# Two-layer transformer kernel: the projection stage taken apart and issued inside the attention program

## What is computed

```python
def _L0_attn_ref(x, w_qkv, w_out, b_out):        # causal attention, 16 heads
    q, k, v = jnp.split(x @ w_qkv, 3, axis=-1)
    ...
    attn = jax.nn.softmax(dots, axis=-1)
def _L0_ffn_ref(x, W_up, W_gate, W_down):
    def ternary_quant(w):
        scale = jnp.mean(jnp.abs(w)) + EPS
        q = jnp.clip(jnp.round(w / scale), -1.0, 1.0) * scale
    ...
def _L1_attn_ref(x, Wq, Wkv, Wo, bo):            # 16 query heads, 4 key heads, linear bias, window mask
    cw = jax.nn.sigmoid(jnp.sum(jnp.abs(x), axis=-1, keepdims=True))
    q = jnp.dot(x * cw, Wq)
    kv = jnp.dot(x, Wkv)
    ...
x = _layernorm(x + _L0_attn_ref(...)); x = _layernorm(x + _L0_ffn_ref(...))
x = _layernorm(x + _L1_attn_ref(...)); x = _layernorm(x + _L1_ffn_ref(...))
```

## Time and profile before

| | before |
|---|---|
| median of three runs | 1176.63 us |
| the profiled execution, its own time | 1173.83 us |
| its span, first to last instruction | 1172.1 us |
| mean granted TensorE clock | 0.942 |
| busy: TensorE, VectorE, ScalarE, GpSimd | 88%, 62%, 51%, 28% |

### The profile page before, as it was taken

The page is one execution under the profiler, slowest core; times in us unless marked ns, Lnnn a source line. Parts: engine busy times, 40 slices in busy tenths (PEclk is TensorE's granted clock), DMA queues, the critical chain, the costliest instruction groups (busy, mean ns, idle before and its releaser), DMA issues. The chain is left out here.

```text
span 1172.1 us, 17910 instructions
## 1 busy us (share of the span) xinstructions
PE 1027.9 (88%) x6546; PEld 516.7 (44%) x6546; DVE 723.9 (62%) x1563; ACT 594.7 (51%) x1169; POOL 323.8 (28%) x391
## 2 busy tenths in 40 slices
PE   7947999999988899765779899999999988899996
PEld 4511233333324788742022333334333334488885
DVE  3767877777734655464878677777777724134322
ACT  3412667666665433234026576767777765523220
POOL 1041111111111343302135613315133150334331
PEclk9966999999999999878569999999999999999998
DMA  7585044444000000008922505235051000000001
GB/s 272 130 155 63 6 51 55 55 55 56 2 1 1 2 1 1 1 19 172 220 102 72 116 2 116 75 42 114 4 117 34 1 2 1 1 1 18 18 1 37
DMA packets 32980, 64.20 MB, mean 55 GB/s; under 512 B 6079, under 2 KB 22351, under 8 KB 30516
## 3 DMA queue, kind: packets, MB, share of 16 engines
q1 hardware_dynamic: 31004, 58.07, 24.9%
q0 software_dynamic: 1072, 3.80, 0.9%
q10 hardware_dynamic: 816, 1.18, 0.3%
HBM read 50.45 MB, written 12.32 MB: 54 GB/s over the span
## 5 line engine op out<-in xcount | busy, mean ns | idle before, releaser
L802 ACT ACTIVATE prob<-ps 128x512 f32<-128x512 f32 (+6 forms) x896 | 445.9, 535 | 306.1 <-PE ps L838 297.9
L838 PE MATMUL ps<-qop,kop 98*128 98x512 bf16 (+15 forms) x1376 | 311.8, 291 | 38.1 <-ACT prob L802 23.0
L824 PE MATMUL ps<-kop,qop 96*128 96x512 bf16 (+3 forms) x896 | 272.6, 380 | 53.1 <-DVE maxes L743 24.7
L838 PEld LDWEIGHTS ps<-qop,kop 107*128 107x128 bf16 (+2 forms) x1376 | 114.0, 98 | 311.7 <-ACT prob L802 236.7
L865 PE MATMUL ps<-prob,vst 128*32 128x512 f32 (+4 forms) x1792 | 212.1, 545 | 3.3 <-POOL prob L692 2.6
L743 DVE CUSTOM_DVE_ANT_0 attn<-ps,alibi_table 128x960 bf16<-128x960 f32 x128 | 148.0, 1156 | 86.6 <-PE ps L824 57.9
L692 POOL TENSOR_TENSOR prob<-prob,keep 128x384 int32<-128x384 int32 (+2 forms) x144 | 122.0, 849 | 276.1 <-ACT prob L802 273.5
L1207 PE MATMUL ps<-xs,ffn_parts 128*128 128x512 f32 x640 | 150.4, 392 | 4.5 <-DVE hf L1181 2.3
L743 DVE CUSTOM_DVE_ANT_0 tri<-ps,alibi_table 128x960 bf16<-128x960 f32 x128 | 147.6, 1153 | 3.0 <-PE ps L824 3.0
L824 PEld LDWEIGHTS ps<-kop,qop 96*128 96x128 bf16 x896 | 77.5, 100 | 143.4 <-DVE maxes L743 84.3
L1207 PEld LDWEIGHTS ps<-xs,ffn_parts 128*128 128x128 f32 x640 | 119.0, 188 | 29.7 <-DVE hf L1181 3.1
(11 more groups left out here) (97 smaller groups left out, 706.5 us busy)
## 6 DMA issues: line engine op xcount, KB each, us to landing
alibi_table<-in_table SPq DMA_DIRECT2D x32, 464.0 KB, 5.6
qop<-q_parts SPq DMA_DIRECT2D x96, 128.0 KB, 7.1
kop<-k_parts SPq DMA_DIRECT2D x48, 128.0 KB, 7.8
kop<-k_parts SPq DMA_DIRECT2D x48, 96.0 KB
q_parts<-qop SPq DMA_DIRECT2D x8, 384.0 KB, 3.0
q_parts<-kop SPq DMA_DIRECT2D x8, 384.0 KB, 6.5
x<-in_x SPq DMA_DIRECT2D x4, 512.0 KB, 7.2
out<-x SPq DMA_DIRECT2D x4, 512.0 KB, 2.9
```

The lines of the kernel that those rows point to most:

```text
L802: nc.scalar.activation(prob[0:rows, q % 2, k % HG, lo % CH:lo % CH + hi - lo], ps[0:rows, T_BANK + k % 2, lo % CH:lo % CH + hi - lo], ACT. ...
L824: last = nc.tensor.matmul(ps[:, S_BANK + 2 * (k % S_SLOTS) + a // CH, a % CH:a % CH + b - a], qop[0:RD, par, h, i0:i0 + P], kop[0:RD, par, ...
L838: return nc.tensor.matmul(ps[0:rows, T_BANK + k % 2, a % CH:a % CH + b - a], lhs, rhs, start=start, stop=True, skip_group_check=True)
```

## The change

`project` and its block are gone. Its steps become a class `Projection`, and each step can be listed in the attention program. `opening_of` writes a new opening: batch 0's turns, units and values first; then group 0's 32 maxima, with batch 1's turns, units and values listed between them. The turned x lies in the buffer of the exponentials. Units, turns and values share three PSUM banks (4 to 6) in turn, where they had eight in three sets. In layer 1 |x| is summed and scaled chunk by chunk. SyncE loads group 0 as soon as units 0 to 3 are in HBM, group 1 after a few more sends (12 in layer 0, 8 in layer 1), and group 2, `wo` and the layer-1 matrices only behind `send_rows(0)`. The bias additions on GpSimd wait for the last turn. In layer 0 the sums and thresholds stay in front (between units 5 and 6), but L421 and L423 move into the last group: one matrix at the end of each of quads 0, 1 and 2, so ahead of "gather".

```diff
@@ plan
+        if last and layer.index == 0 and n < 3:
+            steps.append(("ternary", n, 0))
@@
+def opening_of(layer, proj):
+    first = proj.steps(0)
+    behind = proj.steps(1) + [("flush", 0)]
+    maxima = [("max", u, 1) for u in range(len(units_of(layer)))]
+    if layer.index == 0:
+        at = first.index(("unit", 6))
+        first[at:at] = [("abs", j) for j in range(3)] + [("total", 0), ("threshold", 0)]
+    out = [(what, k, 0) for what, k in first]
+    for n, unit in enumerate(maxima):
+        out.append(unit)
+        upto = [-(-len(behind) * m // (len(maxima) - 2)) for m in (n, n + 1)]
+        out += [(what, k, 0) for what, k in behind[upto[0]:upto[1]]]
+    return out + [("parts", 0, 1), ("rows", 0, 1)]
@@ class Projection
+    BANKS = (4, 5, 6)
...
+            self.units = [(b, m, c) for b in range(B) for p in range(KD) for c in range(2) for m in (p, KD + p)]
...
+        if self.i == 0:
+            vs = [("v", v) for v in range(b * 4, b * 4 + 4)]
+            first = [o for j in range(4) for o in (*units[2 * j:2 * j + 2], vs[j])]
+            return turns + first
+        out = []
+        for j, c in enumerate((2 * b, 2 * b + 1)):
+            out += [("weigh", c), *turns[4 * j:4 * j + 2], ("divide", c), ("scale", c), *turns[4 * j + 2:4 * j + 4]]
+        return out + units + [("v", b)]
...
+        at = self.items.index(step) - len(self.BANKS)
+        if at >= 0:
+            self.wait_read(pe, *self.items[at])
@@ attend, sync
             operands.constants(sp, 0)
             operands.constants(sp, 1)
+            for u in range(4):
+                proj.send(sp, u)
+            proj.wait_sent(sp, 4)
+            operands.load(sp, 0)
+            later = len(proj.units) // 2 + 2 + 2 * (1 - i)
+            for u in range(4, later):
+                proj.send(sp, u)
             operands.load(sp, 1)
-            for k in range(RING):
-                sp.wait_ge(operands.sent[k], K.parts_in_dram[k])
+            for u in range(later, len(proj.units)):
+                proj.send(sp, u)
+            send_rows(0)
+            proj.wait_sent(sp, len(proj.units))
             operands.constants(sp, BUFS - 1)
             operands.load(sp, BUFS - 1)
             sp.dma_start(prep.wo[:], dram.wo[i].rearrange("(k p) n -> p k n", p=P)).then_inc(prep.wo_loaded, 16)
-            send_rows(0)
@@ attend, gpsimd
+            pool.wait_ge(proj.xt_full, len(proj.turns))
             for t in range(NT):
                 nc.gpsimd.tensor_tensor(K.x[:, t, :], K.x[:, t, :], K.bias[:, i, :], ALU.add).then_inc(residual, 1)
@@ attend, tensor
                     elif what == "exp":
+                        if n == 0 and k == 0:
+                            proj.wait_all_read(pe)
@@ build
-                    project(nc, sem, sb, K, L, dram, prep)
                     attend(nc, sem, sb, K, L, dram, prep)
```

More of the change, by code:

```diff
@@ L590, in attend @@
         v_heads = HG if i == 0 else 1
+        maxes = sb(st, "maxes" + tag, [P, HG, TB], F32)
+        sums = [sb(st, f"sums{n}" + tag, [P, T], BF16)[:] if n == 0 or i == 0 else K.tri[:] for n in range(2)]
         vst = sb(st, "vst" + tag, [P, BUFS, TB + i, v_heads, 2 * HD], F32)
@@ L594, in attend @@
         wf = K.staging
-        maxes = sb(st, "maxes" + tag, [P, HG, TB], F32)
-        sums = [attn[:, N - 1, :, :].rearrange("p t d -> p (t d)").bitcast(BF16),
-                sb(st, "sums_odd", [P, T], BF16)[:] if i == 0 else K.tri[:]]
         mpart = sb(st, "mpart" + tag, [P, 2, P // 2], BF16)
@@ L601, in attend @@
         rec = sb(st, "rec" + tag, [P, 2, CT * HG], F32)
-        opening = [("max", u, 1) for u in range(NU)] + [("parts", 0, 1), ("rows", 0, 1)]
+        proj = Projection(nc, sem, sb, st, K, L, dram, prep, prob, K.before_weights)
+        opening = opening_of(L, proj)
         def all_groups(step):
@@ L698, in step @@
                             pool.wait_ge(values_done, group * NQ)
+                        if n == NG:
+                            pool.wait_ge(proj.v_done, (2 - i) * len(proj.v_units))
                         stage(n, n % BUFS)
@@ L781, in step @@
                         ).then_inc(normed, 1)
+                    elif what in Projection.STEPS:
+                        proj.dve(dve, what, k)
                     elif what in Preparation.STEPS:
@@ L811, in step @@
                         nc.scalar.copy(ot[:], ps[:, O_BANK, :]).then_inc(evicted, 1)
+                    elif what in Projection.STEPS:
+                        proj.act(act, what, k)
                     elif what in Preparation.STEPS:
                         prep.act(act, what, k)
+            if i == 0:
+                act.dma_start(proj.w[:], dram.wq[0].rearrange("(k p) n -> p k n", p=P)).then_inc(proj.w_loaded, 16)
+            else:
+                act.dma_start(proj.w[:, :, 0:D], dram.wq[1].rearrange("(k p) n -> p k n", p=P)
+                              ).then_inc(proj.w_loaded, 16)
+                act.dma_start(proj.w[:, :, D:proj.width], dram.wkv.rearrange("(k p) n -> p k n", p=P)
+                              ).then_inc(proj.w_loaded, 16)
+            step(-1, opening)
             all_groups(step)
@@ L928, in step @@
                         last.then_inc(o_turned, 1)
+                    elif what in Projection.STEPS:
+                        proj.pe(pe, what, k)
                     elif what in Preparation.STEPS:
@@ L1275, in build @@
             with ExitStack() as layer:
+                with ExitStack() as early:
+                    if L.index == 0:
+                        K.before_weights = [sb(early, "raw", [P, 3, KD * E], F32)]
+                    else:
+                        K.before_weights = [sb(early, "xct", [P, KD, TOK], F32), sb(early, "xc", [P, CT, D], F32),
+                                            sb(early, "vt", [P, B, T + GLOB], F32),
+                                            sb(early, "wqkv1", [P, KD, D + 2 * L.kv_width], F32)]
                 K.wffn = sb(layer, f"ffn_parts{L.index}", [P, 3, 1 + L.index, KD * E], F32R)
```

542 lines of the change are left out of this document (272 added, 270 removed).

## The result

The changed kernel is slower: 1185.13 us in the median of 18 runs (1180.18 to 1190.86) against 1176.6 of the kernel before (18 runs, 1172.77 to 1184.15); ratio 1.0061, 95% interval 1.0042 to 1.0079. Predicted were 1183.1 and 1174 to 1193. The profiled execution has a span of 1184.9 us against 1172.1. That pair is 12.8 apart where the medians are 8.5 apart: the profiled execution of before, 1173.83 us, is shorter than all but one of its 18 runs, and that of after, 1186.63, is 1.5 above its median.

What follows compares the result with a forecast made beforehand. VectorE was taken to bound both layers' openings, with TensorE nearly always busy elsewhere. Against 1173.83 us, -13.1 + 6.0 + 4.4 + 9.2 = +6.5 gives 1180.3; 2.8 more for the median gives 1183.1, range 1174 to 1193.

Steps and rivals of the forecast that it cites:

- Layer 0 up to E: E, when group 0's first exponential can be fed, comes at 91.5 us instead of 104.59 in layer 0: 13.1 gained.
- the walk: Going through the new step list with profiled durations; in layer 0's opening it came out 5 us above VectorE's own work.
- The clock in layer 0's opening: TensorE, busy without a break in layer 0's opening, was assumed to rise from half to full clock after 5 us.
- rival 3: TensorE's clock stays at half in layer 0's opening, some 20 us more: 1203 us; chance 0.08.
- Layer 0's last group: Two ternary matrices delay the gather; TensorE waits 4.2 us and loses 1.8 to the clock: 6.0 us lost.
- after a gap of this size the clock is at half for about 5 us: Layer 0's last group, behind TensorE's wait for the gather: at most 2.5 us of work lost, 1.8 taken.
- the first of the three: First ternary matrix in layer 0's last group: costed at nothing, since VectorE has 10 idle us there.
- Layer 1 up to the first maximum, and its opening: Layer 1's first maximum 17.6 us earlier, at 542.5; opening 61.8 instead of 39.8; E at 604.3: 4.4 lost.
- The price of the opening: Layer 1's opening: 16.3 us of added VectorE work plus 5.7 us of gaps between TensorE and VectorE.
- The first feed-forward matrix: Layer 1: its DMA, queued behind tables, load 2 and `wo`, lands late and GpSimd waits 7.3 us: 9.2 lost.
- Rival 1: Tables, load 2 and layer 1's first matrix overlap in the queue, so the 9.2 us vanish: 1173.9 us; chance 0.14.
- Rival 2: Loads alone are fast, landing 7.4 us after first issue, in both openings and the matrix: 1172.0 us; chance 0.06.

Runs made afterwards that it cites:

- Experiment 12: Fastest kernel of the study (1156.92 us), with layer 0's feed-forward matrix loads issued after the first four sends landed, their sums behind batch 0's last unit: 1173.11 us.
- Experiments 2 to 4: Changed kernel with ternary matrices moved: all three into group 6, 1176.31 us; all three behind the gather, 1179.64; one ahead and two behind, 1177.02.
- Experiments 9 and 10: Kernel of 1159.45 us (three fixes on the changed kernel), layer 1's six batch-1 units put back between maxima: 1173.82 us; VectorE's unit parts one maximum later: 1164.87.
- Experiment 1: Changed kernel with the DMA of layer 1's first feed-forward matrix issued ahead of load 2 on SyncE: 1174.78 us, ratio 0.9964 to the kernel before.
- experiment 4: Changed kernel with the first ternary matrix left in quad 0 of layer 0's last group, the other two behind the gather: 1177.02 us, ratio 0.9998.

## Why the prediction held, point by point

The forecast came out, and the sum of +6.5 us stands against 8.5 between the medians and 12.8 between the profiled executions. Three of the four terms were right to 0.5 us as sums (13.1 against 12.8, 4.4 against 4.3, 9.2 against 8.8), and the fourth, the last group, was 5 too small. That the median came within 2.0 us is partly luck: the two executions that were profiled lie further apart than the medians.

- **Layer 0 up to E.** Predicted 91.5, measured 91.81; 13.1 us gained, measured 12.8. Two errors of 3 us cancel in it. The first score came at 46.12 and not at 43: the walk left out that a send must land before its part of the ring is written again. The sends shared the DMA engines with 3 MB of matrices, ScalarE stood 4.58 us, and load 0 went out at 30.91 instead of 28.3 (28.1 by the terms of that sum, 25.1 + 3). Experiment 12 shows that cause: without the matrices beside them there is no such wait. The opening was 45.7 and not 48.5.
- **The clock in layer 0's opening** rose as I had let it (0.91 over the whole stretch up to E, where it was 0.80); rival 3 is out.
- **Layer 0's last group.** The mechanism was right (TensorE turns the tile late because VectorE makes two matrices first) and both of its terms were too small: 6.0 us predicted (bounds 4 and 7), 11.1 measured. The turning was to come 4.2 us later and comes 7.3 later. VectorE's 7.3 us for the matrices were nearly right (7.5); left out were that the normalisation itself comes 2.5 later, part of it by the slow clock ahead of it, and that the copy takes longer. The wait is 2.43 and not 4.2 only because TensorE was late itself. And "after a gap of this size the clock is at half for about 5 us", priced at 1.8, was wrong: it took 10.7 to 12.5 us from the turning on until the clock was back, in all four kernels with this order, and 3.8 us were lost. The row I took the 5 us from, shows TensorE after a long opening with nothing in its way; here it was fed by engines that it had to wait for. Experiments 2 to 4 show the loss to hang on the two matrices ahead of the gather, and the first of the three to cost next to nothing, as costed.
- **Layer 1 up to the first maximum, and its opening.** 542.5 and 61.8 predicted, 544.67 and 59.2 measured; E at 604.3, measured 603.83. Here too the parts are off by 2 to 3 us in opposite ways. The predicted times are counted as if layer 1 started where it had, at 502.3, though the sum had it 7.1 earlier; they can be laid beside the measured ones only because layer 0's gain was spent and it started at 502.0. The price of the opening was right: of the 19.4 us more, 15.0 are VectorE's own work (51.47 busy where it was 36.48; 16.3 predicted) and 4.4 are idle time (5.7 predicted). Experiments 9 and 10 show that this isn't given: with the six units spread more thinly VectorE waited 14.0 us for them.
- **The first feed-forward matrix.** 9.2 us predicted, 7.0 + 1.8 = 8.8 measured; GpSimd stood 8.42 us at cut 0 where 7.3 were predicted. The terms given for the landing add up to E + 19.2 and not to the E + 19.9 written there, so to a wait of 6.6; cut 0 began at E + 20.8. Experiment 1 took it away and gave 9.3. Rival 1 is out.
- **Rival 2** (a load is fast when alone) is out: the first score of layer 0 came 15.2 us after load 0's first issue, and waited for it.

What the prediction didn't ask is what batch 1 could do in place of standing between the maxima. It counted VectorE's free time during layer 1's load (16.99 us) nowhere, and that was worth 9.3 us of span.

## What to carry to other kernels

Before work is put between the steps of a busy engine, look for idle time of that engine ahead of them: the same move paid in layer 0 (6.8 us) and lost in layer 1 (13.3), and in these two cases the idle row in front of the first maximum told which. When a step is moved past a queue, follow what was behind it: one DMA issued behind a load instead of ahead of it cost 9.3 us, more than the whole change lost between the medians. Where a step needs three engines in turn, it can pay to list it on the last of them one step later than on the first: here it gave 8.0 and 2.7 us. And a short wait in a trace doesn't mean a small delay: TensorE's 2.43 us in front of the gather hid one of 7.3, since TensorE came late itself. Compare times from the same event in both kernels.

## What the runs showed of the hardware

**The clock can stay at half while TensorE is busy.** From 330 to 355 us in the changed kernel it was at 0.50, with the engine hardly idle in four of the five stretches. Most kernels of the study have a short dip near 330, down to 0.50 to 0.86 in a stretch or two, and those without the three matrices ahead of the gather are back at 1.00 by 345, experiment 4 by 350. In the four with them the clock fell at the latest in the gap in front of the gather. It was back 10.7 to 12.5 us after the turning began, each time during the output projection's matmuls, which follow one another without a pause; until then TensorE stood 0.32 us for an exponential every few matmuls. That order of steps and late return go together is shown, in four kernels against nine. Whether the pauses are why isn't, nor is what starts the dip.

**Two loads at a time.** The last of three feed-forward matrices of 1 MB that GpSimd issues one after another: beside SyncE's sends, in the changed kernel (last column: us to landing), and then beside load 0, in experiment 12:

```profile
raw<-in_down POOLq DMA_DIRECT2D x1, 1024.0 KB, 10.0
```

```profile
raw<-in_down POOLq DMA_DIRECT2D x1, 1024.0 KB, 23.4
```

The first of the three took 5.7 and 12.4 us. It goes both ways: the loads' own DMAs (`qop<-q_parts`, median to landing up to 70 us) took 6.4 us in the changed kernel and 10.4 in experiment 12. Loads with no other transfer beside them move only 118 GB/s, and yet they more than double the time of another queue's transfer. Their share of the engines' time, 1.02 there, is full at that rate, so here the GB/s of a queue was no measure of the room it leaves.
